# One kernel, three edges: the last tile in halves with scales of their own, and a new order around the start of the second FFN

## What is computed

```python
# layer 1, attention of 8 heads without a mask, one batch:
attn = softmax(einsum('bct,bcs->bts', qh * scale, kh * scale))
x = x + tanh(g_xattn) * einsum('bts,bcs->bct', attn, vh)
# layer 1, FFN on the layer norm of x, in blocks of 32 (MX):
#   dequant(t): per block of 32, scale = max|t| / 448, round t/scale to e4m3, times scale
gate = dequant(xn) @ dequant(gate_w).T        # 512 -> 2048
up   = dequant(xn) @ dequant(up_w).T
h    = silu(gate) * up
x = x + tanh(g_ffn) * (dequant(h) @ dequant(down_w).T)   # 2048 -> 512
```

## Time and profile before

| | us |
|---|---|
| three runs | 1504.99, 1511.28, 1515.27 |
| median | 1511.28 |
| profiled execution, its own time | 1508.46 |
| its span on the core | 1506.70 |

### The profile page before, as it was taken

One profiled execution on the slowest core, in us unless ns is written; L12 is line 12 of the kernel. 1 busy time (PEld: TensorE's weight loads), 2 busy tenths in 40 slices (PEclk: granted clock), 3 DMA queues, 4 the chain that ended last, 5 costly groups with the idle time before them and its releaser, 6 DMA issues. The chain is left out here.

```text
span 1506.7 us, 20187 instructions
## 1 busy us (share of the span) xinstructions
PE 1294.6 (86%) x7496; PEld 645.8 (43%) x7496; DVE 1161.6 (77%) x1537; ACT 660.8 (44%) x1048; POOL 475.6 (32%) x346
## 2 busy tenths in 40 slices
PE   4589999376898999883788798889999999999997
PEld 3268777222444444341222122334444444444443
DVE  5567778866888788985777766698888888888875
ACT  3345665256544445434564545233333344333322
POOL 0032341356565566641558687200000000000000
PEclk8899999556999999997899899999999999999999
DMA  8412222347352332234010012310000000000000
GB/s 300 148 62 68 85 80 76 100 144 224 104 153 94 122 117 84 99 112 154 28 42 15 15 52 75 108 61 8 7 14 7 7 7 7 7 7 14 7 8 15
DMA packets 59734, 106.77 MB, mean 71 GB/s; under 512 B 10879, under 2 KB 21783, under 8 KB 59532
## 3 DMA queue, kind: packets, MB, share of 16 engines
q1 hardware_dynamic: 58380, 101.60, 20.7%
q0 software_dynamic: 1280, 4.20, 0.9%
HBM read 73.73 MB, written 27.66 MB: 67 GB/s over the span
## 5 line engine op out<-in xcount | busy, mean ns | idle before, releaser
L1697 PE MATMUL FD<-W0D,HH 128*128 128x512 f16 x512 | 154.6, 384 | 7.0 <-DVE ROOM L1756 3.6
L2555 PE MATMUL HD<-W1H,HT 128*128 128x512 f16 x512 | 154.9, 379 | 0.0
L335 ACT ACTIVATE DD<-E,TM 128x128 f32<-128x128 f32 x256 | 72.9, 370 | 66.6 <-PE E L431 65.0
L1691 PE MATMUL FG<-F,W0G 97*128 97x512 f16 x324 | 83.2, 386 | 20.5 <-PEq L1036 11.2
L2350 DVE TENSOR_REDUCE NQ<-A_M 128x2 f32<-128x1024 f32 x60 | 73.4, 1223 | 35.4 <-PE A_M L2197 35.2
L1622 POOL TENSOR_TENSOR HL<-ROOM,HH 128x512 f16<-128x512 f32 x48 | 76.1, 1586 | 74.8 <-ACT HH L1651 74.8
L1697 PE MATMUL FD<-W0D,HL 128*128 128x512 f16 x256 | 97.9, 383 | 0.0
L2493 ACT CAST OS<-SS 128x2048 f16<-128x2048 f32 x15 | 28.5, 1898 | 156.9 <-DVEq L2630 156.9
L2555 PE MATMUL HD<-W1L,HT 128*128 128x512 f16 x256 | 97.0, 379 | 0.0
L2150 ACT ACTIVATE PT<-A_S,CM 128x1024 f32<-128x1024 f32 x64 | 71.0, 1112 | 56.7 <-PE A_S L2223 56.6
L2608 DVE SCALAR_TENSOR_TENSOR H<-HU,DS,SG 128x512 f32<-128x512 f32 x64 | 48.1, 752 | 58.3 <-ACT SG L2482 54.0
(11 more groups left out here) (382 smaller groups left out, 3040.2 us busy)
## 6 DMA issues: line engine op xcount, KB each, us to landing
VALP<-in_ffn_weights_dram SPq DMA_DIRECT2D x24, 512.0 KB, 4.2
VALQ<-in_ffn_weights_dram SPq DMA_DIRECT2D x24, 512.0 KB, 4.2
quantised_weights<-QQ SPq DMA_DIRECT2D x24, 512.0 KB, 2.7
X<-in_x_dram SPq DMA_DIRECT2D x8, 1024.0 KB, 6.3
W1H<-quantised_weights SPq DMA_DIRECT2D x3, 2048.0 KB, 9.9
F<-features_kept SPq DMA_DIRECT2D x16, 288.0 KB
CTX<-in_ctx_dram SPq DMA_DIRECT2D x4, 1024.0 KB, 7.1
features_kept<-XQ SPq DMA_DIRECT2D x4, 1024.0 KB, 7.0
```

Source lines behind the costliest of these rows:

```text
L335: ins = nc.scalar.activation(DD[:, n % 4, c * P:(c + 1) * P], E[n % 2][:, c * P:(c + 1) * P], ACT.Exp, bias=TM[:, 13 + c, b, h:h + 1])
L1691: last = pe.matmul(banks[t][:, :], GW[rows, t, lhs, cols], F[b % 2][rows, rhs, c, :], start=(n == 0), stop=(n == 2))
L1697: last = pe.matmul(DN[c][:, :], lhs[:, at, c * P:(c + 1) * P], W2[:, i, part, :], start=(i == 0 and n == 0), stop=(i == KI - 1 and n == 2))
L2555: ins = pe.matmul(DN[:, :], HT[:, q, lp, k, :], W[:, 2, i * D:(i + 1) * D], start=(i == 0 and lp == 0 and W is WH), stop=(i == KI - 1 and ...
```

## The change

Attention, quads 6 and 7. The moments of tiles 0 and 1 are taken in quad 6 (MV and SD have two places now), their two square roots stand together at its end. Tile 0 is prepared in one go at step 0 of quad 7, and its low part comes at step 3. The sums of quad 6 are made at step 2 instead of step 6, its reciprocal at step 3, and its spreading in the attention's own block. Tile 0's high part stands on ScalarE one step later, its turning on TensorE too. The last two steps' second additions (`par` 1) move from Pool to VectorE.

FFN1, tiles 0 and 1. The orders of ScalarE and VectorE are written out (`first_silu`, `first_stages`). The sums of quad 7 come ahead of TensorE's first product, the reciprocal ahead of tile 1's preparation, and the normalisations of quads 6 and 7 both behind the third chunk of tile 0. Tile 1 is prepared and turned within the second chunk, tile 2's moments are taken early, and tile 0's H is quantised in halves between the chunks (`quant_first`), with one scale as before.

Last tile. Each half has its own HX and its own scale RSL, is handed on when it is ready, and is multiplied into a bank of its own (`last_products`: half 0 into HG, half 1 into HU), 24 products each; two additions bring them to X. The low part of tile 14 goes ahead of the second chunk's H.

```diff
@@ attention: SyncE, Pool
-                if 0 < g < QUADS - 1:
+                if g:
                     norm.spread(sp, g - 1)
...
-                for par in range(2):
+                shared = k >= STEPS_A - 2
+                for par in range(1 if shared else 2):
@@ attention: ScalarE
+                if g == QUADS - 2 and step == 7:
+                    for tt in range(2):
+                        tokens.deviation(act, tt, tt)
                 if g == QUADS - 1:
-                    if step == 0:
-                        tokens.deviation(act, 0)
-                    if step == 4:
+                    if step == 5:
                         tokens.high(act, 0)
-                    if step == 6:
+                    if step == 7:
                         tokens.turned(act, 0, 0, TX)
@@ attention: TensorE
+                if not more and step == 2:
+                    norm.sums(pe, g - 1)
-                if not more and step == 5:
+                if not more and step == 6:
                     pe.wait_ge(mb_ready, QUADS)
                     tokens.turn(pe, 0, TX)
@@ attention: VectorE
+                    if g == QUADS - 2 and i < 2:
+                        v.wait_ge(x_added, i + 1)
+                        if i:
+                            v.wait_ge(tokens.mv_ready, 1)
+                        tokens.moments(v, i, i)
                     if g == QUADS - 1:
                         if i == 0:
-                            v.wait_ge(x_added, 1)
-                            tokens.moments(v, 0)
                             first = tokens.prepare(v, 0)
                             next(first)
-                        if i == 4:
+                            next(first)
+                        if i == 3:
+                            norm.inverse_sums(v, g - 1)
                             for _ in first:
                                 pass
...
+            s = SS[:, (QUADS - 1) % 2, 3, :]
+            v.wait_ge(pool_own, OWN_BEFORE)
+            for k in range(STEPS_A - 2, STEPS_A):
+                v.wait_ge(p_ready, k + 1)
+                ins = v.tensor_tensor(s, s, PT[:, k % RING, 1, :], ALU.add)
...
+            ins.then_inc(sum_ready, 1)
@@ FFN1: TensorE
-            stage(0, down=False, tail=True)
+            norm.sums(pe, QUADS - 1)
+            pe.wait_ge(xt_taken, 1)
+            for i in range(IC):
+                for t in range(2):
+                    gate_up_products(0, 0, i, t)
+                if i == 1:
+                    tokens.turn(pe, 1, T[0][:, :, :, :])
...
-            stage(TILES + 1, gate_up=False)
+            pe.wait_ge(h_ready, TILES * IC + 2)
+            for half in range(2):
+                turn_hidden(TILES - 1, (2 * half, 2 * half + 1))
+                last_products(TILES - 1, half)
@@ FFN1: VectorE
+            def first_stages():
+                second = tokens.prepare(v, 1, 1)
+                norm.inverse_sums(v, QUADS - 1)
+                next(second)
+                gated(0, 0)
+                for _ in second:
+                    pass
+                tokens.moments(v, 2)
+                gated(0, 1)
+                parts = quant_first()
+                next(parts)
+                gated(0, 2)
+                for g in (QUADS - 2, QUADS - 1):
+                    for q in range(2):
+                        norm.normalise(v, g, q)
+                prepared = tokens.prepare(v, 2)
+                next(prepared)
+                gated(0, 3)
...
```

More of the change, by code:

```diff
@@ L1917, in turn, with moments @@
         ins.then_inc(self.xt_ready, 1)
-    def moments(self, v, tt):
+    def moments(self, v, tt, at=0):
         own = Tally(v, self.s_own, tt, S_OWN)
@@ L2071, in _ @@
                         ins.then_inc(sum_ready, 1)
+                if shared:
+                    continue
                 if j in (1, 2):
@@ L2272, in _ @@
                         negatives(g + 1)
-                    if g:
+                    if g and more:
                         if g % 2 == 1 and b < B:
@@ L2500, in stage, with first_silu @@
                 silu(3)
+            def first_silu(tt, i):
+                act.wait_ge(gu_ready, tt * IC + i + 1)
+                act.wait_ge(h_ready, tt * IC + i + 1)
+                nc.scalar.activation(SG[:, i % 2, :], G[i % 2][:, :], ACT.Silu, scale=DS[:, 0:1]).then_inc(sg_ready, 1)
             act.wait_ge(ds_ready, N_DS)
-            stage(0, quant=False, down=False)
-            stage(1, 1, down=False)
+            first_silu(0, 0)
+            tokens.high(act, 1)
+            first_silu(0, 1)
+            tokens.turned(act, 1, 1, T[0][:, :, :, :])
+            tokens.deviation(act, 2)
+            first_silu(0, 2)
+            first_silu(0, 3)
+            first_silu(1, 0)
+            first_silu(1, 1)
+            act.wait_ge(hv_ready, 1)
+            nc.scalar.copy(HQ[:, 0, :], V[:, :]).then_inc(hh_ready, 1)
+            tokens.high(act, 2)
+            first_silu(1, 2)
+            tokens.turned(act, 2, 0, T[0][:, :, :, :])
+            first_silu(1, 3)
             with act.Fori(2, TILES - 2, 2) as tt:
@@ L2515, in _ @@
                 nc.scalar.copy(HQ[:, 0, cols], V[:, cols]).then_inc(hh_ready, 1)
-            hidden(TILES - 1, (0, 1))
+                if h == 0:
+                    hidden(TILES - 1, (0, 1))
             hidden(TILES - 1, (2, 3))
@@ L2557, in down_products, with last_products, stage @@
                 ins.then_inc(dn_ready, 1)
-            def stage(tt, par=0, gate_up=True, down=True, more=True, tail=False):
+            def last_products(n, half):
+                for q in (2 * half, 2 * half + 1):
+                    pe.wait_ge(ht_taken, n * 4 + q + 1)
+                    for k in range(4):
+                        for lp, W in ((0, WH), (0, WL), (1, WH)):
+                            i = 4 * q + k
+                            first, last = k == lp == q % 2 == 0 and W is WH, k == 3 and q % 2 and lp
+                            ins = pe.matmul((G, U)[half][0][:, :], HT[:, q, lp, k, :], W[:, 2, i * D:(i + 1) * D],
+                                            start=bool(first), stop=bool(last))
+                ins.then_inc(dn_ready, 1)
+            def stage(tt, par=0, gate_up=True, down=True, more=True):
                 if gate_up:
@@ L2574, in stage @@
                             tokens.turn(pe, tt + 1, T[0][:, :, :, :])
-                        if i == 1 and tail:
-                            norm.sums(pe, QUADS - 1)
                         gate_up_products(tt, par, i, 1)
-            stage(0, down=False, tail=True)
+            norm.sums(pe, QUADS - 1)
[5 more added lines that the diff above has]
+                    tokens.turn(pe, 1, T[0][:, :, :, :])
             stage(1, 1, down=False)
@@ new lines, in add_last, with quant_first, step @@
+            def add_last(tt):
+                x = X[:, ds(tt, 1), :]
+                for half in range(2):
+                    v.wait_ge(dn_ready, tt + half + 1)
+                    v.scalar_tensor_tensor(out=x, in0=(G, U)[half][0][:, :], scalar=RSL[:, half:half + 1], in1=x,
+                                           op0=ALU.mult, op1=ALU.add).then_inc((half_added, x_added)[half], 1)
+                    if half == 0:
+                        v.wait_ge(half_added, 1)
+            def quant_first():
+                n, taken = INTER // BLK // 2, [0]
+                def step(ins):
+                    taken[0] += 1
+                    ins.then_inc(first_own, 1)
+                    v.wait_ge(first_own, taken[0])
+                cols = [slice(h * INTER // 2, (h + 1) * INTER // 2) for h in range(2)]
+                rows = [slice(h * n, (h + 1) * n) for h in range(2)]
+                own = Tally(v, first_own, 0, 0)
@@ L2658, in quant_last @@
                     step(v.reciprocal(HI[:, rows[h]], ha))
-                    parts = rounded(v, own, H[:, cols[h]], V[:, cols[h]], M[:, cols[h]], HI[:, rows[h]], n)
-                    next(parts)
-                    if h == 0:
-                        yield
-                    for _ in parts:
-                        pass
+                    own.n = taken[0]
+                    for _ in rounded(v, own, H[:, cols[h]], V[:, cols[h]], M[:, cols[h]], HI[:, rows[h]], n):
+                        if h:
+                            yield
+                    taken[0] = own.n
+                    yield
                 step(v.tensor_tensor(HX[:, 0:1], HX[:, 0:1], HX[:, 3:4], ALU.max))
@@ L2685, in add, with stage @@
                                        op0=ALU.mult, op1=ALU.add).then_inc(x_added, 1)
-            def stage(tt, gate_up=True, quantised=True, down=True, more=True, tail=False):
+            def stage(tt, gate_up=True, quantised=True, down=True, more=True):
                 if gate_up and more:
@@ L2714, in stage @@
                     gated(tt, 3)
-            for q in range(2):
-                norm.normalise(v, QUADS - 2, q)
-            stage(0, quantised=False, down=False, tail=True)
-            v.wait_ge(norm.x_added, 2 * QUADS)
```

(2 more changed lines are left out.)

104 lines of the change are left out of this document (71 added, 33 removed).

## The result

| | us |
|---|---|
| before, median of 20 runs on the same chip | 1515.22 (1504.99 to 1521.48) |
| after, median of 20 runs | 1502.19 (1495.57 to 1511.50) |
| ratio | 0.991, 95% interval 0.9895 to 0.9925 |
| profiled execution of after, its own time | 1497.97 |
| its span on the core | 1496.20 |

The change brings 0.9%: 13.6 us by the ratio (1515.22 x 0.009), 11.4 to 15.9 by its interval. The profile takes them in the three pieces that the prediction named. The windows of after, to be laid beside the earlier trace rows: length, busy PE PEld DVE ACT POOL (instructions), PEclk, DMA share, GB/s.

The account below looks back on a forecast made before the run. TensorE was taken as busy throughout the middle 465.96 us, leaving only the two edges to gain; 2.5 (attention's end) + 5.3 (first two tiles) + 4.7 (last tile) = 12.5 us off 1510.0 gave 1497.5, range 1490 to 1506.

Parts of the forecast that it names:

- Attention's end: End of the attention block: it ends at 940.5 instead of 942.99, a gain of 2.5 us (bounds 0.5 and 3.5).
- Table loads: ScalarE at the end of quad 6: two table loads and two roots take 3.2 us ahead of step 0's exponential.
- The new wait: VectorE in the first tiles: quad 7's transfers, sharing RB with quad 6, take 6.4 us from first issue to use.
- The first two tiles: FFN1's tiles 0 and 1, up to the start of stage 2: a gain of 5.3 us (bounds 2.5 and 9).
- half of tile 2: VectorE's work queued behind quad 7's normalisation, ahead of the fourth chunk's H: 2.7 us, done at 976.9.
- The clock: TensorE's first gate products: 2.0 us lost to a lower clock after the idle time before 941 (bounds 0 and 2.8).
- The last tile: Last tile quantised and multiplied in halves: the end at 1499.3 instead of 1504.00, a gain of 4.7 us.
- The first (only the tail pays): Rival: only the last tile pays, the rest is eaten up; gain 4 to 8 us, 1502 to 1506; chance 0.17.
- The second (more than summed): Rival: no clock fall, additions free of Pool, silu not late, copies overlapped; gain 15.5 to 18 us; chance 0.14.
- The third (a lasting low clock): Rival: TensorE stays at 1.2 GHz through tiles 0 and 1, making it slower, up to about 1520; chance 0.04.
- The fourth: Rival: nothing gained at the last tile, VectorE's last half still sets the end; gain 7.8 us, 1502; chance 0.05.
- "same": Outcome for the whole kernel: a change within about 1% (15 us), given 0.66, beside faster 0.30 and slower 0.04.

Follow-up runs that it names:

- e6: The changed kernel with ScalarE's cast of tile 0 put back at the last quad's step 4, as in the kernel before; one run, 1497.66 us.
- e5: The changed kernel with 11 idle products added on TensorE behind the attention's last product, their result read by nothing; one run, 1507.00 us.
- e9: The changed kernel with a buffer of its own for quad 7's factors, VectorE's order untouched; one run, 1505.88 us.
- e3: The changed kernel with quad 6's two normalisations moved ahead of the first chunk's H of tile 0; 1494.47 us, ratio to before 0.9869.
- e7: The changed kernel with ScalarE's cast of the last tile's first half put between the two pairs of copies of the tile before; one run, 1505.27 us.
- e2: The changed kernel with the last tile's old order; 1507.38 us, ratio to before 0.9963.
- e1: The kernel before with only the last tile's new order; 1507.91 us, ratio to before 0.9965.
- e10: The changed kernel with quad 6's normalisations ahead of tile 0's H, the last tile's cast between copies and its turns between products; 1500.07 us, ratio to before 0.9885.

## Why the prediction was right, point by point

The forecast was a gain of 12.5 us, to 1497.5, in a range of 1490 to 1506. The medians give a gain of 13.0 and 1502.19; the difference in the level is that of the base, which the prediction took as 1510.0 and the twenty runs now give as 1515.22.

- **Attention's end, 2.5 forecast.** From A the block's end came 2.7 earlier (943.59 - 890.22 = 53.37 against 942.13 - 891.46 = 50.67; both are the first TensorE row behind the barrier). The sum is right, and it has the cause in it: it lets VectorE finish the tile at 930.8, where ScalarE's cast had stood until 933.0. What its account had wrong is the place of the cast, which it took with it ("it has only been put where its data is ready"); e6 shows that putting it there is worth nothing, since VectorE brings the tile 2.5 us earlier in either place. That the size came out as well is partly luck, as two sizes cancelled beside it: the additions took 2.48 us together, not 3.3, and the second normalisation, beside Pool, 1.76, not 1.3. And the transfers of quad 6, which the sum has done 0.8 us before the additions, ended with them (941.30 and 941.26). The additions by line in after (duration in ns, lowest, median and highest):

```profile
L2437 DVE TENSOR_TENSOR SS<-SS,PT x2: 693/1221/1749, 938.8 to 940.6; 128x512 f32<-128x512 f32 x2
```

The first, beside Pool's (until 939.98), took 1.75 us, the second, when Pool was done, 0.69: the prediction took Pool's company for both. Quad 6's slots are late by 0.24 us (the products of step 55 start 24.90 us behind A in before, at 915.12, and 25.14 in after, at 916.60; 0.2 in all the traces with the new order but e6), 0.4 was charged.
- **Table loads.** 916.31 (load) to 919.40 (exponential) are 3.09 us for two loads and two roots, 3.2 forecast. ScalarE's timeline of after:

```profile
916.31 1.28 ACT L1901 ACT_TABLE_LOAD   x1
917.61 0.48 ACT L1901 ACTIVATE SD<-MV,EPS 128x1 f32<-128x1 f32 x2
918.11 1.28 ACT L2156 ACT_TABLE_LOAD   x1
```

The Trainium skill, "ScalarE: Activation LUTs", What ACT_TABLE_LOAD costs, has about 2.66 us for each; by it the pair alone would be 5.3, an estimate. The trace of after agrees with the 1.28 us of the earlier trace rows instead.
- **The new wait, 6.4 forecast.** From the first issue of quad 7's transfers to the use of the second half: 967.83 to 974.23, 6.40 us; that it repeats isn't sure, as e5 took 7.67 (975.59 to 983.26). e9 and e3 show its cause. VectorE's waits of 3.29 and 1.90 are as named (3 and 2), TensorE's 5.66 is over the 4.6 given.
- **The first two tiles, 5.3 forecast.** 4.6 by the window lengths (61.63 in the earlier trace rows, and 942.13 to 999.16 = 57.03). The failed term is "half of tile 2 (2.7: 976.9)": it took 3.68 (974.84 to 978.52), because L1935 ran 1.51 us instead of 0.55 at the moment of Pool's residual addition (975.00 to 976.26, Pool's timeline). That collision was costed at nothing, as an idle Pool's work.
- **The clock, 2.0 forecast.** The trace of after has it: 3.57 us for the first eight, 1.7 over the full-clock 1.9. The idle products of e5 and the trace of e7 show that it was the wrong thing to attach it to: the slow group can come two chunks later, and its place is worth 1.0. In after itself the charge fits: the first H starts 10.19 us behind the first row after the block (952.32 and 942.13), the forecast has 10.2 (951.3 and 941.1). That the slow group fell there, as in four of the ten traces, is luck. The transfer of W1L's half was costed at nothing as lying beside the first chunk; that held in after, where the first products were slow, and in the six traces where they were fast TensorE waited for it.
- **The last tile, 4.7 forecast.** 4.6 (35.7 and 31.1). Products of 5.35 and 5.37 us (5.2 forecast), two waits of 0.66 (0.85), VectorE's wait for the cast 2.69 (3). That the wait would cost nothing is shown by e7.
- **The rivals.** The first (only the tail pays) is out: e2 gains without the tail. The second (more than summed) gave 1492 to 1494.5, and the gain of 11.4 to 15.9 us touches its lower end of 15.5 only just; of its parts, one of the two additions was free of Pool, and the clock's fall was there. The third (a lasting low clock) is out: G to T has a granted clock of 0.91, before had 0.89. The fourth is out: e1. The Trainium skill, "SBUF — State Buffer", Who interferes with whom, has an exclusive lock, which the prediction turned into 1.94 us for an operation of VectorE beside Pool. The longest two of after at the block's end, 1.76 and 1.75 us, lie between that and the 1.65 of the earlier trace rows.

The chances gave "same", within 1%, 0.66, and that is where 0.9% falls, near its edge.

## What to carry to other kernels

When a consumer of a buffer is moved back, look who must write the buffer next: here the late normalisation of quad 6 held quad 7's transfers for 21 us, and 5.2 us of waits stood on the path for it. A buffer of its own won back 3.2 of them, as the work then ran beside Pool's; putting the read into a wait that was there anyway won 6.5. Before crediting a move with the wait that it removes, ask whether the awaited data comes earlier by the rest of the change; then the move itself is worth nothing. And where the work ahead of a change scatters by more than the change is worth, compare traces from a mark just ahead of it.

## What the runs showed of the hardware

- **Slow products wander.** With the same instructions and the same idle time (3.24, 3.23, 3.27 us) before them, the first eight gate products took 3.57 us in after, 1.90 in e7, 1.90 in e10; in the latter two a group of the third chunk took 3.12 and 3.13 instead of 1.89, behind an idle time of 2.19 and 3.07 us. Which group pays differs from trace to trace, and it is one of the two in all ten traces with the new order.
- **Much of the spread is made early.** A lies between 890.2 and 903.5 in the twelve traces, though nothing ahead of it was changed; behind it, stretches with the same code differ by 1.4 us at most. The traces are of different kernels on several chips, so how much of the spread between one kernel's runs on one chip arises before A isn't shown, and what makes it is open.
- **VectorE beside Pool.** A 128x512 addition took 1.75 us beside Pool's additions and 0.69 alone, a multiplication 1.76 and 0.69, and a tensor_scalar with one such input 1.51 and 0.55: the operation with one input lost 0.96 us, those with two 1.06 and 1.07.
